# A graph-attention kernel on one core: edges placed in list order, and 3 tiles in 16 picked by TensorE from 256 loaded table rows instead of gathered

## What is computed

```python
def setup_inputs(seed=0):
    x = normal((6250, 128)); src, dst = randint(200000, 0, 6250), randint(200000, 0, 6250)
    _o = jnp.argsort(dst, stable=True); src, dst = src[_o], dst[_o]
    edge_attr_64 = normal((200000, 64))
# layer 0: five rounds of a graph convolution over src -> dst (h @ W, scaled segment sum, batch norm, leaky)
# x = layernorm(x + layer 0)
# layer 1, with row, col = src, dst:
Q, K, V = nodes @ wq + bq, nodes @ wk + bk, nodes @ wv + bv          # 8 heads of 16
scores = (Q[row] * K[col]).sum(-1) / 4 + (Q[row] * (edge_attr @ we + be)).sum(-1) / 4
es = exp(scores); denom = segment_sum(es, row)
out = segment_sum(es / (denom[row] + 1e-8) * V[col], row) @ wo + bo
# result: layernorm(x + out)
```

## Time and profile before

| what | value |
|---|---|
| times of three executions | 6985.19, 7047.67, 7072.9 us |
| span of the profiled execution | 4521.0 us |
| granted TensorE clock, mean | 0.961 |
| busy: PE, DVE, ACT, POOL | 3433.8, 2826.2, 1260.5, 3265.7 us |
| chain that ended last, by engine | POOL 54%, issue 23%, DVE 8%, DMA 7%, PE 1% |
| loads of a group's records, gathers | 404, 1616 |

### The profile page before, as it was taken

How to read it: one execution, slowest core, us unless ns; L and a number is a source line. 1 busy time by engine, 2 the same in 40 slices (tenths; PEclk the granted TensorE clock), 3 DMA queues, 4 the chain that set the end, 5 groups by cost and what they waited for, 6 DMA issues and landing times.

```text
span 4521.0 us, 79418 instructions
## 1 busy us (share of the span) xinstructions
PE 3433.8 (76%) x22509; PEld 2392.6 (53%) x22510; DVE 2826.2 (63%) x7836; ACT 1260.5 (28%) x2975; POOL 3265.7 (72%) x3278
## 2 busy tenths in 40 slices
PE   5568787699999999999955776676776766666664
PEld 3234444344545444454434666666666666666664
DVE  8999999311313113131155787878788888888887
ACT  0056666300101001010043333333333333333331
POOL 2177878777777777777777777777777777777772
PEclk8989999899999999999978999999999999999998
DMA  9425546799998999989934444444444444444442
GB/s 374 180 102 201 191 172 215 258 355 331 311 356 300 356 329 319 356 286 353 332 113 118 132 131 131 133 130 131 132 131 133 130 131 132 131 130 132 131 130 69
DMA packets 359548, 927.62 MB, mean 205 GB/s; under 512 B 68946, under 2 KB 186654, under 8 KB 357574
## 3 DMA queue, kind: packets, MB, share of 16 engines
q1 hardware_dynamic: 196086, 549.20, 35.1%
q0 software_dynamic: 132752, 280.95, 21.0%
q10 hardware_dynamic: 30656, 96.86, 6.5%
HBM read 726.32 MB, written 200.41 MB: 205 GB/s over the span
## 4 chain that ended last, share of the span: by engine, by line
POOL 54%; issue 23%; DVE 8%; DMA 7%; PE 1%; DVEq 1%; POOLq 0%; ACT 0%
POOL records L993 36%; POOL kv L1630 17%; DMA kv<-kv_table,rec 7%; DVE msg L1728 2%; DVE kq L1720 2%; DVE kq L1719 2%; PE ps L1665 1%; DVE h L1742 1%; POOL recs L975 0%; DVEq L1564 0%; DMA records<-recs,pos 0%; DVE deg L1841 0%; POOL recs L976 0%; DVE st_f L1827 0%; DVE scores L1723 0%
## 5 line engine op out<-in xcount | busy, mean ns | idle before, releaser
L993 POOL DMA_INDIRECT records<-recs,pos x1562 | 1627.5, 1042 | 476.1 <-issue 470.7
L1630 POOL DMA_INDIRECT kv<-kv_table,rec x1616 | 1549.8, 959 | 496.6 <-issue 430.6
L1115 PE MATMUL ps<-adj,mh 128*128 128x500 f16 (+1 forms) x6370 | 1311.8, 367 | 17.4 <-DVE mh L1266 16.5
L1115 PEld LDWEIGHTS ps<-adj,mh 128*128 128x128 f16 x6370 | 620.0, 97 | 687.7 <-DVE mh L1266 17.3
L1665 PE MATMUL ps<-msg,ohf 128*128 128x136 f32 x3232 | 489.1, 295 | 634.6 <-DVE msg L1728 634.5
L1665 PEld LDWEIGHTS ps<-msg,ohf 128*128 128x128 f32 x3232 | 407.6, 192 | 709.6 <-DVE msg L1728 354.3
L1287 DVE TENSOR_TENSOR adj<-adj,quarter 128x128 f16<-128x128 f16 (+25 forms) x305 | 46.0, 209 | 772.3 <-DMA adj<-adj_full 764.0
L1695 ACT ACTIVATE msg<-scores 128x32 f32<-128x32 f32 x404 | 92.6, 229 | 1285.7 <-DVE scores L1723 1285.7
L1654 PE MATMUL ps<-qn,oht 128*128 x3232 | 441.2, 281 | 0.3 <-ACT at L1688 0.2
L1657 PE MATMUL ps<-we,at 128*128 128x128 f32 x3232 | 432.5, 277 | 0.0
L1654 PEld LDWEIGHTS ps<-qn,oht 128*128 128x128 f32 x3232 | 407.4, 198 | 1.0 <-issue 1.0
(11 more groups left out here) (255 smaller groups left out, 3750.5 us busy)
## 6 DMA issues: line engine op xcount, KB each, us to landing
adj<-adj_full SPq DMA_DIRECT2D x420, 875.0 KB, 5.9
adj_full<-blk SPq DMA_DIRECT2D x12, 6125.0 KB
records<-deg ACTq DMA_DIRECT2D x1, 56576.0 KB, 163.0
rec<-records SPq DMA_DIRECT2D x404, 136.0 KB
recs<-in_edge_attr ACTq DMA_DIRECT2D x27, 1408.0 KB, 14.9
kv<-kv_table,rec POOLq DMA_INDIRECT x1616
records<-recs,pos POOLq DMA_INDIRECT x1562
adj<-adj_tail SPq DMA_DIRECT2D x35, 437.5 KB, 4.7
```

What stands on the lines that cost most here:

```text
L993: G.indirect_dma_start(out=k.rec_d, out_offset=bass.IndirectOffsetOnAxis(ap=k.pos[:, at:at + 1], axis=0), in_=k.recs[:, q, j, :], in_offse ...
L1115: last = mm(bank, mh[:, part, hi, :], adj[:, c, x * width:(x + 1) * width], start=(hi == 0 and part == 0), stop=True, skip_group_check=True)
L1630: G.indirect_dma_start(out=kv[:, q, j, :], out_offset=None, in_=k.kv_d, in_offset=bass.IndirectOffsetOnAxis(ap=rec[:, q, j, RD:RD + 1].bit ...
```

## The change

Four things are changed.

1. *Order.* Edges are read so that the place within a block follows the list. For this the places of 12 squares of 128 x 128 edges are turned by TensorE before they are used, the attributes are loaded in the same squares (`STEPS`: 37 steps instead of 36; `OWN` = 10 of them are issued by POOL instead of 9), and `src` is loaded once more. A row count of descents in `dst` (`falls`) tells whether the list is sorted.
2. *Picks.* In tile 0 of the groups with q = 0, 1, 2 (3 tiles of the 16 of a quad) K and V are not gathered. SP loads 256 rows of `kv_table` from the tile's first `dst` on (`load_window`); VectorE marks for each edge which of the rows it wants (`spot`), TensorE turns that and multiplies it with the rows, for K into the same PSUM bank as the projected attributes, for V into another, and ScalarE brings both to SBUF (`lift_keys`, `lift_values`).
3. *Fallback.* A tile is *good* if the list is sorted and its last `dst` is less than 256 rows above its first. A tile that is not good is multiplied by 0. If not every first tile of the 416 groups is good, a loop behind the main loop (`again`) goes over all picked tiles of all quads, three for each, with a gather, and multiplies the good ones by 0.
4. *VectorE.* The four one-hot instructions of a group are one on 16-bit pairs, the four message instructions are one. The records are loaded as rows of 68 words instead of pairs of rows, since tile j is now 128 consecutive rows.

Beside these, some semaphores are shared by several purposes, and the loads of loop counts and of the window table lose the argument that skips a bounds check.

```diff
+PICKS = (0, 1, 2)
+ROWS = 2 * P
@@ prepare
-                sp.dma_start(src_n[:, 0:TF], io["src"][0:full].rearrange("(p c) -> p c", p=P)).then_inc(got_s, 16)
+                sp.dma_start(src_n[:, 0:TF], io["src_cols"]).then_inc(got_s, 16)
...
+                for x in range(SQUARES):
+                    last = nc.tensor.transpose(PS[:, 4 + x // 4, x % 4 * P:(x % 4 + 1) * P], posf[:, x * P:(x + 1) * P], k.ident[:, :])
...
-                L(V.tensor_copy(k.dl[:, :, 1].bitcast(FP32), i1[:, :]))
+                L(V.tensor_copy(k.dl[:, :, 1:2].bitcast(BF16), i1[:, :].rearrange("p (c o) -> p c o", o=1).broadcast_to([P, TC, 2])))
+                v.wait_ge(squares_turned, 1)
+                V.tensor_copy(k.pos[:, 0:TURNED].rearrange("p (b c) -> p b c", c=512), PS[:, 4:4 + TURNED // 512, :])
...
+                L(V.scalar_tensor_tensor(falls, order[0:WP, 0:ORDER - 1], 0.0, order[0:WP, 1:ORDER], ALU.add, ALU.is_gt,
+                                         accum_out=found[0:WP, 11:12]))
@@ attend
+        def again(eng, engine, what):
+            most = nc.values_load(k.gb[0:1, LEAD + NPR + 11:LEAD + NPR + 12], engines=(engine,), min_val=0, max_val=NQ)
+            with eng.Fori(0, most) as i:
+                for x, q in enumerate(PICKS):
+                    what(eng.snap(i * R + q), eng.snap(i * len(PICKS) + x))
...
+            def load_window(g, q):
+                at_ = nc.values_load(based[:, bass.ds(g, 1)], engines=(ENG.SP,), min_val=0, max_val=NP - ROWS, ...)
+                sp.dma_start(window[:, PICKS.index(q), :, :],
+                             k.kv_d[bass.ds(at_, ROWS), :].rearrange("(p o) c -> p o c", o=2)).then_inc(wl[PICKS.index(q)], 16)
+            def load_again(g, n):
+                by_dve(sp, "started", n)
+                sp.dma_start(rec[:, 0, 0, :], k.rec_d[bass.ds(g * GE, P), :]).then_inc(R_["loaded"], 16)
...
-                    for j in range(GT):
+                    for j in range(GT - gathered(q), GT):
+                        gather(q, j, kl[q])
...
+            def pick_values(g, q, i):
+                if q not in PICKS:
+                    return
+                before(pe, "messages", g, S)
+                added(pe, g, 2 * S)
+                x = PICKS.index(q)
+                for h in range(2):
+                    last = mm(PS[:, 6 + q % S, VALUE], spot_t[:, q % S, h, :], window[:, x, h, D:2 * D], start=(h == 0), stop=(h == 1))
+                last.then_inc(picked, 1)
-            steps(pe, ENG.PE, ((sums, 4), (turn, 0), (query, 1)), query)
+            steps(pe, ENG.PE, ((turn_spots, 1), (pick_values, 2), (sums, 4), (turn, 0), (query, 1)), query)
...
-            steps(act, ENG.Activation, ((pack, 0), (evacuate, 1), (weigh, 2)))
+            steps(act, ENG.Activation, ((lift_keys, 2), (pack, 0), (evacuate, 1), (weigh, 2), (lift_values, 2)))
...
+            L(V.tensor_tensor(far, padded, some, ALU.mult))
+            L(V.tensor_tensor(far, far, last_, ALU.add))
+            L(V.tensor_scalar(base, first, float(NP - ROWS), None, ALU.min))
+            L(V.tensor_tensor(far, far, base, ALU.subtract))
+            L(V.tensor_scalar(far, far, float(ROWS), None, ALU.is_lt))
+            L(V.tensor_scalar(good, far, k.gb[0:1, LEAD + NPR + 10:LEAD + NPR + 11].bitcast(FP32), None, ALU.mult))
+            L(V.tensor_reduce(total[:, 0:1], good, AX.X, ALU.add))
+            L(V.tensor_scalar(total[:, 0:1], total[:, 0:1], NG - 0.5, None, ALU.is_lt))
+            V.tensor_tensor(k.gb[0:1, LEAD + NPR + 11:LEAD + NPR + 12], total[:, 0:1], k.gb[0:1, LEAD + NPR + 8:LEAD + NPR + 9], ALU.mult)
```

More of the change, by code:

```diff
@@ L15 @@
 P = 128
+ORDER = 1600
 N = 6250
@@ L81, in entry @@
 def entry(nc, engine, table, at, low, high):
-    return nc.values_load(table[0:1, bass.ds(at, 1)], engines=(engine,), min_val=low, max_val=high,
-                          skip_runtime_bounds_check_because="the program has made the table within these bounds")
+    return nc.values_load(table[0:1, bass.ds(at, 1)], engines=(engine,), min_val=low, max_val=high)
 class Chain:
@@ L1583, in steps @@
             for q in range(R):
[L1584 removed]
+                one(0, 0, q, (lambda x: first[x]) if block_op else None, lambda x: x >= 0)
             with eng.Fori(1, quads) as i:
@@ new lines, in sp_att @@
+            for n, r in enumerate((0, P - 1)):
+                sp.dma_start(ends[:, n, :, :].bitcast(FP32), rows[:, r:r + 1, RD:RL + 1].rearrange("g r w -> r g w")).then_inc(ends_loaded, 16)
+            def load(row, q):
+                sp.dma_start(rec[:, q, :, :], k.rec_d[bass.ds(row, GE), :].rearrange("(t p) c -> p t c", p=P)).then_inc(rl[q], 16)
+            def load_window(g, q):
+                at_ = nc.values_load(based[:, bass.ds(g, 1)], engines=(ENG.SP,), min_val=0, max_val=NP - ROWS,
+                                     skip_runtime_bounds_check_because="the program has clamped them")
+                sp.dma_start(window[:, PICKS.index(q), :, :],
+                             k.kv_d[bass.ds(at_, ROWS), :].rearrange("(p o) c -> p o c", o=2)).then_inc(wl[PICKS.index(q)], 16)
@@ L1656, in query, with sums @@
                 for j in range(GT):
-                    last = mm(PS[:, 4 + q % S, j * P:(j + 1) * P], at[:, q % S, j // 2, :], we[:, j % 2, :], start=True, stop=True)
+                    chosen = q in PICKS and j == 0
+                    last = mm(PS[:, 4 + q % S, j * P:(j + 1) * P], at[:, q % S, j // 2, :], we[:, j % 2, :], start=True, stop=not chosen)
+                    if chosen:
+                        x = PICKS.index(q)
+                        pe.wait_ge(wl[x], 16 * i + 16)
+                        for h in range(2):
+                            mm(PS[:, 4 + q % S, 0:P], spot_t[:, q % S, h, :], window[:, x, h, 0:D], start=False, stop=(h == 1))
                 last.then_inc(S_["queried"], 1)
-            def sums(g, q):
+            def sums(g, q, i):
                 done(pe, "messages", g)
                 done(pe, "onehot_f", g)
-                before(pe, "added", g, S)
+                added(pe, g, S)
                 for j in range(GT):
@@ L1693, in weigh, with lift_values @@
+            def lift_values(g, q, i):
+                if q not in PICKS:
+                    return
+                act.wait_ge(picked, nth(q, i))
+                added(act, g, S)
+                before(act, "messages", g, R)
+                act.sem_inc(sem("rec_gated"), 1)
+                A.activation(kv[:, q, 0, D:2 * D], PS[:, 6 + q % S, VALUE], ACT.Identity, scale=goodcol[:, bass.ds(g, 1)]).then_inc(lifted, 1)
+            def weigh(g, q, i):
                 done(act, "scored", g)
```

393 lines of the change are left out of this document (289 added, 104 removed).

## The result

| | median, us | lowest to highest | runs |
|---|---|---|---|
| kernel before | 7054.6 | 6985.19 to 7072.9 | 4 |
| changed kernel | 9485.4 | 9483.78 to 9497.4 | 4 |

The changed kernel takes 1.346 times as long (95% interval 1.339 to 1.354), 2431 us more. The forecast was 10,060 us in a range of 9300 to 10,700.

What follows compares the result with a forecast made beforehand. POOL bounds the main loop at 5.06 us for a group, the VectorE-TensorE ring close behind at 4.92. Span 4521 + 30 - 45 + 3030 = 7536 us; median 7048 + 3015 = 10,063, predicted 10,060 us, range 9300 to 10,700.

Steps and rivals of the forecast that it cites:

- The loop runs, and makes 303 turns.: Loop behind the main loop: one bad tile, in group 398, makes it run 101 x 3 = 303 turns; chance 0.84.
- A turn takes 10.0 us.: Loop behind the main loop: each turn is a serial chain of 10.0 us, 3030 us in all, between 2610 and 3420.
- the lower bound of 8.6 for the turn: Loop behind: shortest turn expected, with POOL starting 0.30 us after the load, faster sums and shorter landings: 8.6 us.
- The ring becomes 4.95 us, POOL falls behind it, gain 45 us.: Main loop: VectorE-TensorE cycle of messages, sums, additions and scores goes 4.92 to 4.95 us, POOL 5.06 to 4.11; 45 us gained.
- The value picks' +0.33 us: Main loop: two float32 products ahead of TensorE's sums, 0.45 us in three groups of four, add 0.33 us on average.
- The other terms of the ring: Main loop, VectorE: one message instruction saves 0.20 us for a group, the shorter addition of K on average 0.10.
- Paid once 30 us.: Outside the loops: preparation +10 us, one more scatter step's wait +5, window table and first loads +15; together +30.
- The part outside the span stays as it is.: Whole execution: the 2527 us by which the timed median exceeds the profiled span were taken as unchanged.
- the first: Rival for the loop behind: it does not run, giving 7033 us, or 6694 with POOL as the bound; chance 0.16.
- POOL as the bound: Rival for the main loop: POOL still sets the pace, gaining 384 us, and the loop behind runs: 9724 us; chance 0.13.
- A ring of 5.5 us: Rival for the main loop: picks lengthen the VectorE-TensorE cycle to 5.5 us, 178 us lost: 10,286 us; chance 0.13.

Runs made afterwards that it cites:

- run 101: No run has this name: 101 is the number of quads, 404 groups in all, that the loops go over.
- The run that begins the loop at the first bad quad: Changed kernel with VectorE's first addition behind the scores and the loop behind begun at the first quad with a bad group: 4320.31 us, ratio 0.9553.
- the changed kernel's second trace: The changed kernel without edit, on a chip where the kernel before takes 4522 us: 7067.02 us, ratio 1.5618.
- the ring taken apart: VectorE's first addition moved behind the scores, in the kernel before (4535.99 us) and the changed kernel with 14 (4376.73) or 13 gathers (4302.62, loop count 0).
- the old order with 14 gathers: Changed kernel with two picked tiles in 16 instead of three, VectorE's first addition still ahead of the scores: 4502.81 us, ratio 0.9959 to the kernel before.

## Why the prediction came out as it did

The sign, the mechanism and the range were right. By its steps:

- *The loop runs, and makes 303 turns.* Right. The run that begins the loop at the first bad quad makes 6 turns, that is two rounds of 101 quads counted from 0, so that quad is 99, where group 398 stands.
- *A turn takes 10.0 us.* This is the term that was mis-sized: 8.39 us measured, 2542 us instead of 3030. Against the pieces taken from the earlier trace rows: load until ScalarE 1.77 instead of 2.30, gather's end to the first score 1.97 instead of 3.43, the rest within 0.1 us in sum. The 3.43 came from a row with four gathers in flight, and I took off only 0.5 us for load and gather together. The 8.39 us lie below the lower bound of 8.6 for the turn; the range of the whole time held because other terms had room. The estimate from the Trainium skill, "DMA: Bandwidth & Descriptors", section "Anatomy of one DMA" (2.3 us for such a gather) gave a turn of 7.9 us and lay nearer. The trace doesn't agree with its 2.3 us either: from the gather's start to the first score it is 0.95 + 1.97 = 2.92 us here.
- *The ring becomes 4.95 us, POOL falls behind it, gain 45 us.* Right: 4.96 us against 5.06, 38 us in the main loop. The value picks' +0.33 us is 0.334 by doubling them. The new sum for a group with a pick, 4.92 - 0.20 + 0.45 - 0.13 = 5.04, is 5.02 in the row. The other terms of the ring weren't tested one by one.
- *Paid once 30 us.* 40 us: first additions begin at 2457.9 instead of 2417.5. The size is near, the reason was another. The waits of ScalarE at the convolution's start, in the trace of the kernel before and in the changed kernel's second trace, neither of which has stops:

```profile
ACT h L1138 <- DMA records<-recs,pos: 14.4, 1, 14.4
```

```profile
ACT h L1177 <- DMA records<-recs,pos: 77.9, 1, 77.9
```

ScalarE issues the attribute loads from step `OWN` on, ahead of its first activation, and that load waits for the scatters of two steps earlier. Before that was step 7, 22 + 7 x 44 = 330 scatters; now it is step 8, 3 x 128 = 384. The first such load goes out at 885.1 instead of 816.0 us, the convolution's last matmul starts at 2320.9 instead of 2266.2, and POOL then waits 30 us for records that SP may load only behind it (`h_taken`), where it waited 4.4. So the first gather starts 29 us later (2430.35 against 2400.92), and from it to the first addition it takes another 11 us. I counted the scatters' own end, which is only 4 us later. This is read from the traces; a run with `OWN = 9` wasn't made.
- *The part outside the span stays as it is.* The number held (2527 us before; 9485 - 7067 = 2418 us for the changed kernel), the picture didn't. For the changed kernel the 2418 us lie inside the span: 1777 us ahead of the first addition of the main loop (4234.9 against 2457.9), 640 us in the main loop, and 3 in the loop behind. That the 2527 us of before are stops of the same kind is inferred from their size; no execution of it with such a time has a trace. Nothing in the prediction gave a reason why the two kernels should have nearly the same amount, so this term came out right by luck.
- *The rivals.* The loop ran, so the first falls. POOL as the bound falls in the old order; it needs the ring taken apart, which no rival had. A ring of 5.5 us falls with 4.96.

10,060 against 9485 is 575 us. The terms give 580: 303 x (10.0 - 8.39) = 488 us of the turn and 109 us of the part in stops, less 17 us of the small ones (10 more paid once, 7 less gained in the main loop). The other 5 us are rounding and the difference between medians and profiled executions.

## What to carry to other kernels

A path for rare data must cost by how rare it is: here a count of "all or none" turned one bad tile into 2542 us, and starting the loop at the first bad quad made that 50. Before work is taken off a busy engine, walk the ring that stands behind it once round and ask which step could run in another's shade: here 3 gathers in 16 were worth 0.1 us for a group, and 0.73 us once one addition had moved behind three instructions. When the size of a transfer step changes, look at which other engine issues those transfers in its own stream.

## What was not expected of the hardware

- The same kernel before took 7050 us where it was first timed and 4521 to 4528 us on the chips of the experiments; the changed kernel 9485 and 7067. In the changed kernel's first trace several engines stop together for 5 to 19 us, in the scatters, the convolution and the main loop, but not in the loop behind, which takes 2544 us there and 2542 us on the other chip. In the main loop they come once in each round of the loop, and TensorE's granted clock is 0.50 for 3 to 7 us behind each. The loop behind moves 20 GB/s, the main loop 115. What stops them stays open.
- A loop with a count of 0 made one round (3 turns of three picks, 2 of two); what makes the round wasn't looked into.
- One copy of 128 x 2 numbers by POOL at the start of the scatters (`rec_tail`) takes 3.45 us in some profiles and 54.85 in others, of the same program lines. It doesn't cost 51 us: where the copy is short, the first scatter behind it takes 41 to 45 us, and where the copy is long, that scatter takes 1.1 to 1.5 us, so some 45 to 50 us are spent once in either place. In the profiles of the changed kernel's forms the second scatter starts about 12 us later with the long copy, and the first addition of the attention 17 to 22 us later; that accounts for differences of this size between the runs above. In the profiles of the kernel before's forms the first addition differs by 5 us at most. The executions of the old order with 14 gathers fall into two groups at such a distance, five from 4501 to 4504 us and two at 4521.
- With one gather in flight its rows are used 1.97 us after POOL's row ends; with four it was 3.43 us.
